# Float32r head scores in two halves of the TensorE array, with a head's output finished by ScalarE and GpSimd

## The reference

```python
q, k, v = (split_heads(x @ w + b) for w, b in ((sq_w, sq_b), (sk_w, sk_b), (sv_w, sv_b)))
scores = einsum('bqhd,bkhd->bhqk', q, k) / sqrt(16)
probs = softmax(scores, axis=-1)                     # over 1024 keys
out = einsum('bhqk,bkhd->bqhd', probs, v)
```

## Time and profile before

| | us |
|---|---|
| median of 3 runs | 1222.73 (1219.84 to 1222.77) |
| profiled execution, its own time | 1223.43 |
| span of its profile | 1221.7 |
| TensorE busy (matmul records) | 1101.5 |
| VectorE busy | 829.6 |
| ScalarE busy | 610.7 |
| GpSimd busy | 285.8 |

### The profile page before, as it was taken

How to read it: one execution, slowest core, us unless ns; L and a number is a source line. 1 busy time by engine, 2 the same in 40 slices (tenths; PEclk the granted TensorE clock), 3 DMA queues, 4 the chain that set the end, 5 groups by cost and what they waited for, 6 DMA issues and landing times.

```text
span 1221.7 us, 20881 instructions
## 1 busy us (share of the span) xinstructions
PE 1101.5 (90%) x7648; PEld 603.6 (49%) x7648; DVE 829.6 (68%) x1453; ACT 610.7 (50%) x1159; POOL 285.8 (23%) x651
## 2 busy tenths in 40 slices
PE   6699689858999999999999889894989999999998
PEld 3366356502333333333333445663678877667665
DVE  1568658777888888888887327645374576987665
ACT  2265256406676766767667522130223345656643
POOL 3211212000100101001001124327238554621010
PEclk7799889958999999999999988987999999999999
DMA  7302100261122121221211331001015431110000
GB/s 193 55 11 70 60 2 23 91 196 61 34 68 60 39 63 34 69 62 35 63 34 40 126 105 35 9 9 69 27 57 178 148 100 44 39 35 2 12 11 31
DMA packets 102851, 73.34 MB, mean 60 GB/s; under 512 B 50738, under 2 KB 93791, under 8 KB 102495
## 3 DMA queue, kind: packets, MB, share of 16 engines
q1 hardware_dynamic: 99679, 63.61, 17.8%
q0 software_dynamic: 3072, 8.39, 2.1%
HBM read 42.94 MB, written 28.84 MB: 59 GB/s over the span
## 4 chain that ended last, share of the span: by engine, by line
PE 74%; DVE 13%; ACT 4%; issue 3%; POOL 2%; DMA 2%; SPq 1%; DVEq 0%; ACTq 0%; POOLq 0%
PE OUT L782 14%; PE TR L782 14%; PE OUT L1003 12%; PE SCR L992 9%; PE TR L788 8%; PE SCR L950 5%; PE TR L950 5%; PE TR L892 2%; PE OUT L788 2%; PE SCR L876 2%; ACT PTS L1239 2%; DVE small L1430 2%; PE SCR L869 2%; DVE small L1545 1%; POOL dispatched L1977 1%
## 5 line engine op out<-in xcount | busy, mean ns | idle before, releaser
L1283 ACT ACTIVATE shared<-SCR 128x512 f32<-128x512 f32 x512 | 277.8, 594 | 113.7 <-PE SCR L992 112.7
L1545 DVE TENSOR_REDUCE small<-TR 128x1 f32<-128x1024 f32 x128 | 156.8, 1225 | 48.9 <-PE TR L950 46.4
L1545 DVE TENSOR_REDUCE small<-SCR 128x1 f32<-128x1024 f32 x128 | 156.6, 1223 | 22.0 <-PE SCR L950 18.4
L1003 PE MATMUL OUT<-shared,HM 128*32 128x256 f32 x2048 | 163.7, 391 | 0.4 <-ACT shared L1283 0.4
L992 PE MATMUL SCR<-shared 99*128 99x512 bf16 x512 | 157.0, 382 | 4.7 <-DMA shared<-MT 4.4
L1856 POOL TENSOR_SCALAR small<-small 128x1 f32<-128x1 f32 x112 | 28.2, 252 | 398.1 <-DVE small L1431 396.4
L782 PE MATMUL TR<-xT,fifo 128*128 128x512 f32 x224 | 113.1, 665 | 2.8 <-ACT xT L1219 2.8
L950 PE MATMUL TR<-shared 96*128 96x512 bf16 x256 | 81.1, 400 | 15.4 <-DMA shared<-pieces 13.6
L1901 POOL CAST small<-small 128x8 bf16<-128x8 f32 x32 | 7.4, 231 | 371.4 <-DVE small L1545 371.4
L1219 ACT ACTIVATE xT<-TR 128x256 f32<-128x256 f32 x96 | 35.6, 382 | 115.8 <-PE TR L788 115.2
L1003 PEld LDWEIGHTS OUT<-shared,HM 128*32 128x32 f32 x2048 | 40.3, 108 | 102.7 <-issue 98.8
(11 more groups left out here) (236 smaller groups left out, 1816.4 us busy)
## 6 DMA issues: line engine op xcount, KB each, us to landing
pieces<-shared SPq DMA_DIRECT2D x16, 384.0 KB, 2.5
shared<-pieces SPq DMA_DIRECT2D x64, 96.0 KB
HM<-dispatched SPq DMA_DIRECT2D x46, 128.0 KB, 2.2
expert_out<-HM SPq DMA_DIRECT2D x46, 128.0 KB
dispatched<-HB SPq DMA_DIRECT2D x6, 768.0 KB, 3.7
shared<-pieces SPq DMA_DIRECT2D x64, 64.0 KB
shared<-in_L_ffn_w SPq DMA_DIRECT2D x4, 1024.0 KB, 10.7
X<-in_x SPq DMA_DIRECT2D x1, 2048.0 KB, 9.0
```

The source lines that it names most:

```text
L1003: ins = nc.tensor.matmul(PV[32 * g:32 * g + 32, 0:256], VH[:, j % 2, kt, :], PTB[:, kt % 2, g * 256:(g + 1) * 256], start=(kt == 0), stop= ...
L1283: nc.scalar.activation(PTB[:, kt % 2, hf * 512:(hf + 1) * 512], SCR[:, bank, :], ACT.Exp, scale=DH ** -0.5).then_inc(st_done.sem, 1)
L1545: nc.vector.tensor_reduce(nm[:, r, kt:kt + 1], pair.rearrange("p h n -> p (h n)"), AX, ALU.max, negate=True)\
```

## The change

Each of q and k is now held in two parts of type float32r (a 32-bit type, which part c's last product uses already) instead of three in bfloat16: a head has 3 x 16 = 48 rows, and 51 with the maxima. Rows 0 to 63 of QX and KX hold one head and rows 64 to 127 another, two buffers of each, so four heads are loaded. Heads n and n+2 always lie in different halves, and TensorE's order alternates a `t_scores` matmul of head n with a `max_scores` matmul of head n+2. In QK VectorE has one subtraction left for each block. QX and KX lie beside what part a uses, so the first four heads are loaded at the start of part a's second pass; the rows of ones are stored once by DMAs in the setup.

ScalarE now copies the transposed maxima to MT and the transposed output to OT; GpSimd makes the reciprocal as a power of -1 and the product. The signs of the ternary weights are made on GpSimd, by three operations (four with the scale) for each piece, and VectorE has only the reductions in part b. The heads are one loop with no end of a group at every fourth head.

```diff
-QROWS = 6 * DH
+QROWS = 3 * DH
...
-        PC = shared[:, o:o + 3072].bitcast(BF16).rearrange("p (e c n) -> p e c n", e=4, c=3)
         PTB = shared[:, o:o + 2048].rearrange("p (r n) -> p r n", r=2)
+        PC = [over(f"pieces_{e}", [128, 2, N], F32R, "shared", o + 1024 * e) for e in range(2 * KD - 1)]
         o += 3072
+        QX, KX = ([over(f"{name}_{r}", [128, S], F32R, "shared", o + 1024 * (2 * r + c)) for r in range(2)]
+                  for c, name in enumerate(("head_q", "head_k")))
+        o += 4096
...
-        MT = sb("MT", [24, 128], BF16)
+        MT = over("MT", [24, 128], F32R, "QT")
...
-        scratch = nc.dram_tensor("pieces", [2, 3, NH * DH, S], BF16)
+        scratch = nc.dram_tensor("pieces", [2, 2, NH * DH, S], F32)
...
+        def half(n):
+            return 64 * (n // 2 % 2)
...
+                for r in range(2):
+                    for g in range(0, 128, 64):
+                        for c in range(3):
+                            sp.dma_start(KX[r][g + QROWS + c:g + QROWS + c + 1, :].bitcast(F32).rearrange("p (q t) -> p q t", t=128),
+                                         ones_rows[c * 8:c * 8 + 8, :]).then_inc(d_ones, 16)
+                def load_head(n):
+                    src = scratch[:, :, n * DH:(n + 1) * DH, :]
+                    q, k, g = QX[n % 2][:, :].bitcast(F32), KX[n % 2][:, :].bitcast(F32), half(n)
+                    sp.dma_start(q[g:g + 2 * DH, :], src[0, 0].unsqueeze(0).to_broadcast([2, DH, S])).then_inc(d_head[n % SLOTS], 16)
+                    sp.dma_start(k[g:g + 2 * DH, :], src[1]).then_inc(d_head[n % SLOTS], 16)
+                    sp.dma_start(q[g + 2 * DH:g + 3 * DH, :], src[0, 1]).then_inc(d_head[n % SLOTS], 16)
+                    sp.dma_start(k[g + 2 * DH:g + 3 * DH, :], src[1, 0]).then_inc(d_head[n % SLOTS], 16)
...
+                    if b > 0:
+                        sp.wait_ge(d_pieces, DC + 16 * 4 * BLOCKS)
+                        for n in range(SLOTS):
+                            load_head(n)
...
-                pair = SQ[tl.slot(sq_full, 2)]
-                tl.next(sq_full)
-                pe.wait_ge(sq_done.sem, tl.back(sq_full, 2))
-                for hf in range(2):
-                    ins = nc.tensor.matmul(pair[:, hf, :], QX[j][0:QROWS, kt * 128:(kt + 1) * 128],
-                                           KX[j][0:QROWS, hf * 512:(hf + 1) * 512], start=True, stop=True)
-                ins.then_inc(sq_full.sem, 1)
...
+            def max_scores(tl, n, kt, hf):
+                if hf == 0:
+                    tl.next(sq_full)
+                    pe.wait_ge(sq_done.sem, tl.back(sq_full, 2))
+                rows = slice(half(n), half(n) + QROWS)
+                ins = nc.tensor.matmul(SQ[kt % 2][:, hf, :], QX[n % 2][rows, kt * 128:(kt + 1) * 128],
+                                       KX[n % 2][rows, hf * 512:(hf + 1) * 512], start=True, stop=True)
+                if hf == 1:
+                    ins.then_inc(sq_full.sem, 1)
+            def t_scores(tl, n, kt, hf):
+                bank = tl.slot(st_full, 2)
+                tl.next(st_full)
+                pe.wait_ge(st_done.sem, tl.back(st_full, 2))
+                rows = slice(half(n), half(n) + QROWS + 3)
+                nc.tensor.matmul(SCR[:, bank, :], KX[n % 2][rows, kt * 128:(kt + 1) * 128],
+                                 QX[n % 2][rows, hf * 512:(hf + 1) * 512], start=True, stop=True)\
+                    .then_inc(st_full.sem, 1)
...
+            for n in range(NH):
+                pe.wait_ge(d_m2, (n + 1) * 48)
+                if n + 2 < NH:
+                    pe.wait_ge(d_head[(n + 2) % SLOTS], 16 * 4 * ((n + 2) // SLOTS + 1))
                 for kt in range(QT_PER_HEAD):
-                    if kt == 0:
-                        pe.wait_ge(d_m2, (n + 1) * 48)
-                    t_scores(kt)
+                    for hf in range(2):
+                        t_scores(tl, n, kt, hf)
+                        if n + 2 < NH:
+                            max_scores(tl, n + 2, kt, hf)
                     if kt > 0:
-                        values(kt - 1, 2)
-                    elif rest:
-                        rest(2)
-                    if kt == 2 and not (last and j == UNROLL - 1):
-                        maxima_transpose(tl, (j + 1) % 2, n + 2)
-                    if kt == 4 and j >= 1:
-                        head_out_transposes(tl)
-                    if not (last and j >= 2):
-                        if kt == 0:
-                            pe.wait_ge(d_head[(j + 2) % UNROLL], (i + (1 + (j + 2) // UNROLL)) * (16 * 6))
-                            max_scores(tl, (j + 2) % UNROLL, 0)
-                        if rest or kt > 1:
-                            if kt > 0:
-                                max_scores(tl, (j + 2) % UNROLL, kt)
-                        elif kt == 0:
-                            max_scores(tl, (j + 2) % UNROLL, 1)
-                if j < UNROLL - 1:
-                    return lambda ahead: values(QT_PER_HEAD - 1, ahead)
-                values(QT_PER_HEAD - 1, 0)
...
+                        values(tl, n, kt - 1, 2)
+                    elif n > 0:
+                        values(tl, n - 1, QT_PER_HEAD - 1, 2)
+                    if kt == 3 and n + 1 < NH:
+                        maxima_transpose(n + 1)
+                    if kt == 5 and n >= 1:
+                        head_out_transposes(n - 1)
...
+            def transposed_output(n):
+                act.wait_ge(aux_full.sem, taken["out", n])
+                act.wait_ge(oh_ready.sem, n)
+                nc.scalar.activation(OT, AUX[:, 0:256], ACT.Copy).then_inc(aux_done.sem, 1)
+            def maxima_rows(n):
+                act.wait_ge(aux_full.sem, taken["max", n])
+                act.wait_ge(d_m2, n * 48)
+                nc.scalar.activation(MT[:, :], AUX.bitcast(BF16)[0:24, 0:128], ACT.Copy).then_inc(aux_done.sem, 1)
...
-                    rest = HM[:, 2, :]
                     for e in range(2 * KD):
                         dve.wait_ge(tr_done.sem, tl.next(tr_done))
-                        chain(nc.vector.tensor_tensor(rest, RR[:, e % 2, :], PC[:, e, 0, :], ALU.subtract))
-                        chain(nc.vector.tensor_copy(PC[:, e, 1, :], rest))
-                        nc.vector.tensor_tensor(PC[:, e, 2, :], rest, PC[:, e, 1, :], ALU.subtract)\
+                        nc.vector.tensor_tensor(PC[e][:, 1, :], RR[:, e % 2, :], PC[e][:, 0, :].bitcast(F32), ALU.subtract)\
...
-            def maxima_rows(tl, stored):
-                bank = aux_filled(tl)
-                dve.wait_ge(d_m2, stored)
-                nc.vector.tensor_copy(MT[:, :], bank.bitcast(BF16)[0:24, 0:128]).then_inc(aux_done.sem, 1)
-            def head_out(tl, chain, n, r):
-                bank = aux_filled(tl)[:, 0:256].rearrange("p (s g d) -> p g s d", s=2, g=4)
-                rs = rsum[:, 0:8].rearrange("p (g s) -> p g s", s=2)
-                chain(nc.vector.reciprocal(rs, bank[:, :, :, DH]))
-                dve.wait_ge(d_oh[r], (n // 2) * 16 + DC)
-                nc.vector.tensor_tensor(OH[:, r, :, :].rearrange("p (g s) d -> p g s d", s=2),
-                                        bank[:, :, :, 0:DH],
-                                        rs.unsqueeze(3).to_broadcast([128, 4, 2, DH]), ALU.mult)\
-                    .then_inc(aux_done.sem, 1)
-                dve.wait_ge(aux_done.sem, tl.value(aux_full))
             tl = Tally("b0")
...
+            def ternary(tl, chain, w, m, scaled):
+                below = TN[:, 0:w.shape[-1]]
+                chain(nc.gpsimd.tensor_scalar(below, w, wscale[:, 2, m:m + 1], None, ALU.is_lt))
+                chain(nc.gpsimd.tensor_scalar(w, w, wscale[:, 1, m:m + 1], None, ALU.is_gt))
+                ins = nc.gpsimd.tensor_tensor(w, w, below, ALU.subtract)
+                if scaled:
+                    chain(ins)
+                    ins = nc.gpsimd.tensor_tensor(w, w, wscale[:, 0, m:m + 1].to_broadcast([128, D]), ALU.mult)
+                ins.then_inc(tern_ready.sem, 1)
...
+            def head_out(n):
+                pool.wait_ge(aux_done.sem, taken["out", n])
+                pool.wait_ge(d_oh[n % 2], (n // 2) * 16 + DC)
+                v = OT.rearrange("p (s g d) -> p g s d", s=2, g=4)
+                rs = rsum[:, 0:8].rearrange("p (g s) -> p g s", s=2)
+                chain(nc.gpsimd.tensor_tensor(rs, v[:, :, :, DH], minus_one.unsqueeze(2).to_broadcast([128, 4, 2]), ALU.pow))
+                nc.gpsimd.tensor_tensor(OH[:, n % 2, :, :].rearrange("p (g s) d -> p g s d", s=2), v[:, :, :, 0:DH],
+                                        rs.unsqueeze(3).to_broadcast([128, 4, 2, DH]), ALU.mult)\
+                    .then_inc(oh_ready.sem, 1)
...
+                i = n // 4
+                if n % 4 == 0:
+                    ternary(tl, chain, wfc[:, i, :], i, True)
+                elif n % 4 >= 2:
+                    ternary(tl, chain, wproj[:, n % 4 - 2, i * 128:(i + 1) * 128], MF + n % 4 - 2, False)
```

(64 more changed lines are left out.)

280 lines of the change are left out of this document (94 added, 186 removed).

## The result

The change makes the kernel slower: 1300.88 us in the median of 4 runs (1292.95 to 1315.14) against 1222.75. A run over 1.5% above the fastest of its kernel, as the one of 1315.14 is, is left out of every comparison of two kernels: the other three have a median of 1297.69, ratio 1.061, 95% interval 1.054 to 1.068. Predicted were 1152.4 us and a range of 1130 to 1190. The profiled execution took 1292.95 us, its span is 1290.9.

A forecast was written before the change was run, and what follows sets the result against it. The prediction took TensorE to bound part b's heads; 59.4 - 1.0 - 0.9 + 10.5 + 3.0 = 71.0 us off the profiled 1223.4 gave 1152.4 us, with a range of 1130 to 1190.

The forecast's parts named there:

- (1): Part b's score matmuls: halves and weight loads overlap, four cost about two; TensorE 1.20 us a tile, 10.1 a head.
- (2): ScalarE's two added copies in part b: 10.9 us a head instead of 12.88, a gain of 59.4 us.
- B: Rival for part b: weight loads don't overlap, 12.8 to 12.9 us a head, 1212 us in all; chance 4%.
- C: Rival for part b: the halves don't overlap at all, 13.6 us a head, 1233 us in all; chance 3%.
- A: Rival for part b: coupling of ScalarE, TensorE and VectorE costs more, 11.7 us a head, 1176 us; chance 16%.
- Part (4): From part a to the first head: operands loaded earlier, first `t_scores` at 269.6 us, a gain of 10.5 us.
- (5): Part a's other three QK steps: fewer VectorE operations per block, a gain of 3.0 us, between 0 and 6.
- Part (3): GpSimd's added work in part b: some 5 us of 10.9 a head, nobody waits; 0.9 us lost at the end.
- Rival D: Part b: two score streams together leave TensorE little work, clock falls to 1.2 GHz, 16.2 us a head, 1311 us; 5%.

The follow-up runs named there:

- experiment 1: The kernel after the change, but SyncE stores the output of head n-2 where it stored that of head n-1: 1167.67 us, ratio 0.957.
- experiment 3: The kernel of experiment 1 with `values` between both `t_scores` and both `max_scores`, as before the change, so the halves don't overlap: 1235.06 us, ratio 1.012.

## Why the prediction was wrong

*Parts (1) and (2), right.* The halves overlap, with weight loads in parallel. Heads 29 and 30 of the kernel after, which run at full clock without a stop, take 11.1 us, one with `max_scores` and one without, and all heads but the first of experiment 1 take 11.09, where 10.9 was predicted within 10.3 to 11.7. Rivals B and C fall. A's coupling shows in part: a tile is 1.39 us, with ScalarE idle for 0.2 of it. The tile of experiment 1 that is shown takes 1.25 us (0.34 and 0.35 from pair to pair to `values`, 0.56 for these), where I had 1.20. With the pair at 0.28, the estimate from the Trainium skill, "TensorE: Matmul & The Clock Gate", Part 3, it would be 1.32. ScalarE and VectorE set the pace too, so this trace can't price the pair.

*A slip in the rows.* What the earlier trace rows calls the first `t_scores` of heads 30 and 31 are the second ones. The first start at 665.35 and 675.43: behind each of them come the last `values` of the head before, and behind these ScalarE's copy of its output (line 1276, at 666.74 and 676.86).

```profile
665.35 0.60 PE L992 MATMUL SCR<-shared 99*128 99x512 bf16 x2
...
675.43 0.79 PE L992 MATMUL SCR<-shared 99*128 99x512 bf16 x2
```

So a head of before took 12.84 us and not 12.88, and head 30 took 10.08 and not 10.28. With the right rows the working gives 10.08 + 0.59 = 10.7 us a head and some 5 us more gain. That the forecast of 10.9 lies within 0.2 of the measured 11.09 is luck in part, and the coupling costs 0.4 us a head, less than half of what A would have from 10.7 to 11.7.

*Part (4), right in sign.* The first `t_scores` is at 264.1 instead of 280.1, 16.0 earlier; (4) and (5) had 13.5 together. The weights came 8 us after their issue, not 14.5, so the reductions of b0 decide.

*Part (3), the step that failed.* "Nobody waits: the output's way has a whole head." The next sentence named the mechanism ("a late head_out would hold ... SyncE's queue, with the next head's load behind it") and left it at nothing, without laying the instants side by side. They could be worked out from the program alone: the product of head n-1 stands behind `head_values`, which needs the last `values` of head n, made in head n+1; SyncE's order has that store ahead of head n+1's load and rows. So load and rows leave late and back to back. That the power takes 1.65 us rather than 0.60 added some 31 us, and the place the rest. The 0.60 had been read from an operation on one element in each partition, and this one has eight.

*Rival D, right in kind, 5%.* The clock is what made it slower: 49% of the heads' time at 1.2 GHz, 1293 us in the profiled execution against D's 1311 and its threshold of 45%. But D's reason, that two columns stream together, is not what happened (experiment 1: 1.00). The evidence I set against it, heads 30 and 31 of before, was sound for a stream without stops and said nothing on a stream with them. Two things were missing: a stop as the trigger, and a slow return. Its price was low too: a slow tile is 2.16 us, not 1.95, and a head of slow tiles 18.0 (482.6 to 500.6 us), not 16.2.

*The sum after the fact.* Experiment 1 shows the change as I had pictured it: 1167.67 us, 15 over the forecast and within the range. Its profiled execution has a span of 1160.1, where the working gives 1221.7 - 71.0 = 1150.7. Of these 9.4 us, 30 x 0.19 = 5.7 are the heads and 3.9 is head 0, which runs at 1.2 GHz for the most part (clock 0.59) and takes 15.0 instead of 11.1; 2.0 come back, as head 0 starts at 264.6 and not at 280.1 - 13.5 = 266.6. Another 1.1 is the slip in the rows (666.44 - 665.35), and the last 0.7 lies behind the start of head 30 and isn't placed. The 130 us from experiment 1 to the kernel after are the stops and the slow clock: in the profiled executions 128.4 of them lie in the heads up to the last (475.9 against 347.5), and 46.8 of these are waits for the rows.

## What to carry to other kernels

Where a piece of work moves to another engine, write down for each queue that waits on it when it will be ready and what is queued behind the wait, in instants and not in engine shares; a DMA queue that is in order turns one idle-looking store into a late load. Price a stop of TensorE at more than its length, and try a new stream with a stop put in before you trust its clock. When a change loses though its own part shows the gain, look for the single wait that undoes it: here one index in SyncE's order was worth 130 us.

## What the runs showed of the hardware

- The clock behind a stop differs from kernel to kernel. Stops of 1.5 to 3.4 us: 3.4 us at 1.2 GHz, sometimes 6.8, in the bfloat16 kernel. Stops of 2.1 us: 3.4 to 41.0 us at a time in the overlapped float32r kernel, and no return at all over 714 us without the overlap, at stops of 2.2 that came every 23.9 us. Stops of 1.4 us left the bfloat16 kernel at 0.99.
- A TensorE that is busy in the records can stay at 1.2 GHz for long: without the overlap the float32r kernel ran 47.9 us so, with 47.7 of them busy and no stop (experiment 3).
- Longer stops were not always worse for the clock: the overlapped kernel was granted 0.69 with stops of 2.1 us and 0.73 with 3.4, though it was slower in time.
- Float32r matmuls of 51 and 48 rows in different halves start within 0.01 us of each other, 512 columns each, and their loads (0.18 us) too.
- GpSimd's power on 128 x 8 elements took 1.65 us, an addition there 0.20.
- Three DMAs for 24 rows of 512 bytes issued directly behind a head's load of 384 KB were there 7.5 us after their first issue (555.47 to 563.0), 0.5 us behind the load, and 3.2 us after it where the load was issued behind them (370.03 to 373.21).
